# Moving the placement of dtu by one decay, loading all expert rows at once, and 32 matmuls ahead of the last stage of a Mamba and mixture-of-experts kernel

## The chip, the cores and the metric

The kernel runs on one core of a Trainium2 chip (trn2). The metric is the device time of one execution in microseconds. Three executions of the kernel before took 2603.61, 2604.18 and 2603.98 us, so the median is 2603.98. All data are float32.

## What is computed

Input `x` has 32 sequences of 128 tokens with 128 features. Four things follow one another; cut to what matters:

```python
# 1. adapter per sequence (its language picks the weights), then layer norm
x1 = norm(x + relu(x @ W1[id] + b1[id]) @ W2[id] + b2[id]) * gamma[id] + beta[id]
# 2. four Mamba layers, d_inner 256, state 16
for i in range(4):
    xs, z = split(layer_norm(x1) @ Wi.T)
    u = silu(causal_conv4(xs) + cb)
    dt, B, C = split(u @ Wx.T);  dt = softplus(dt @ Wdt.T + bdt)
    h[t] = exp(dt[t] * A) * h[t-1] + dt[t] * u[t] * B[t];  y[t] = h[t] . C[t]
    x1 = ((y + u * Dp) * silu(z)) @ Wo.T + x1
x = x + x1
# 3. dense experts: 8 gated by fside, one shared, each (silu(x Wg) * (x Wu)) Wd
y = (1 - sg) * sum_e p[e] * expert_e(x) + sg * shared(x)
# 4. sparse experts, top 2 of 8 by y @ wg, capacity 1024 rows each
out = x + g1 * ffn_e1(y) + g2 * ffn_e2(y)      # ffn: gelu(row @ w_gate) @ w_down
```

## The kernel before

`mega` calls three phases: `wave_phase` (1 and 2, and the dense experts of half of the tokens woven in), `dense_phase` (the dense experts of the other half, and the routing), and `sparse_phase` (4). Each is one block of code with a program for each of the engines PE, ACT, DVE, POOL and SP (SP only issues DMAs). Engines run their own program in the order in which it is written, and meet through counting semaphores. At the end of a block there is a drain of each engine and a semaphore round of all.

**The wave.** Tokens are in 8 groups of four sequences (512 columns). An iteration `i` (0 to 31) is one layer of one group, and has 16 steps `k`, each for two of the 16 states of one half of the channels. In a step ACT makes the decays (`decay`, L715: two exponentials, at most four steps ahead of the scans), DVE multiplies `dtu` in PSUM by B (`input_term`, L882) and scans (`scan_step`, L893), POOL multiplies by C (`weigh_states`, L1030), and PE adds the states up in PSUM (`sum_states`, L452). In between, by the tables `PE_AT`, `ACT_AT` and `POOL_AT`, which name a piece of work for a step `k`, the next iteration is prepared. On ACT the pieces of a step stand ahead of its decay. `dtu` (dt times u) of the next iteration is made by POOL at step 11 (`time_input`, L1012), and in the first half (iterations below `RING0` = 13) ACT copies its two channel halves into the banks `psT[0]` and `psT[1]` (`place_dtu`, L683): half 0 as `dtu0` at step 15 of the iteration before, half 1 as `dtu1` at step 1 of its own. Half 0's bank has been free since the middle of the iteration before, half 1's only after its last scan. The copy of half 0 waits for POOL's `dtu`. DVE's input term of step 0 waits for the copy.

**The end of the dense phase.** After the last group's experts come its routing on PE and DVE (`post`, `ranks`, `slots`), a small matmul into `psN` (L1324), and on POOL eight indirect DMAs (`scatter`, L1217) that write the last group's rows into `disp` in DRAM. `disp` has two arrays (first and second choice) of 8 experts by 1024 rows of 132 numbers: the token, its index and its weights.

**The sparse phase.** SP loads both arrays' rows of an expert into `dx[0]` and `dx[1]` (`load_rows`, L1518 and L1520; 528 KB each, expert 0's in halves), in a ring of three experts (`NDX`), so expert `e` from 3 on waits until expert `e-3` has been weighed (`evac`). Experts 0 and 1 have their weights loaded in the dense phase; the others' stand in the ring of two (`load_weights`, L1525 and L1526). An expert is two halves of 512 rows. For each half DVE picks rows from the two arrays (`pick`, L1621), PE transposes (`turn`, L1560), DVE copies (`turned`, L1633), PE multiplies by `w_gate` (`up`, L1570), ACT takes the gelu (L1607), PE multiplies by `w_down` (`down`, L1578), and DVE scales by the routing weight into `eos` (`weigh`, L1644). POOL then adds the rows to `out` in DRAM by eight indirect DMAs an expert (L1546), 128 rows each, and waits at the start of an expert until all DMAs of the expert before have landed (`added`), as two experts can add to the same token.

## Time and profile before

| | us |
|---|---|
| median of three runs | 2603.98 |
| the profiled execution | 2603.44 |
| its span, first to last instruction | 2601.7 |
| PE busy (matmuls) | 2318.5 (89%) |
| DVE busy | 2055.6 (79%) |
| POOL busy | 2045.6 (79%) |
| ACT busy | 1555.7 (60%) |
| DVE scans, 512 of 2.283 us | 1165.7 |
| POOL products by C, 512 of 2.36 us | 1205.4 |
| ACT decays, 1024 of 0.708 us | 667.4 |
| POOL scatters into `out`, 64 of 1.555 us | 99.5 |

Busy shares are means over stages with different limits: the wave lasts to 2047 us, the dense phase to about 2437, the sparse phase to the end. PE's busy time counts matmuls that are pipelined, with modelled ends. In rows of a timeline the numbers are the start, the duration of the merged instructions, the engine, the line, the operation with its output and inputs, how many instructions are merged (x), and in brackets the idle time of the engine before them and what ended it.

### The profile page before, as it was taken

To read this page: it belongs to the slowest core of one execution; us is meant where nothing else is said; L and a number is where in the kernel's file an instruction comes from. 1 tells how busy PE (TensorE), PEld (TensorE's weight loads), DVE (VectorE), ACT (ScalarE), POOL (GpSimd) and SP (SyncE) were. 2 spreads that over 40 slices of the span, in tenths; PEclk is the share of its full clock that TensorE was granted. 3 is DMA by queue.
4 is the path that set the end of the run, shared out by engine and by line. 5 is a ranking of instruction groups with operands and counts; after the bars stand their busy time and mean duration, and the time that the engine had idled before them with its cause. 6 is when DMAs were issued, how large, how long until landed. Compare 5 with 4: busy or idle time off the path is not lost. (4 is left out here: it accounts for less than half of the span.)

```text
span 2601.7 us, 22564 instructions
## 1 busy us (share of the span) xinstructions
PE 2318.5 (89%) x6064; PEld 1023.4 (39%) x6064; DVE 2055.6 (79%) x2028; ACT 1555.7 (60%) x2432; POOL 2045.6 (79%) x1269
## 2 busy tenths in 40 slices
PE   6588888888888999999999999999998899999594
PEld 4233333333333333343443333333333344444373
DVE  4799999999999999999999999999999343333221
ACT  3576777776777677777766767777765223222221
POOL 4599999999998899999999999999999332321366
PEclk9799999999999999999999999999999999999797
DMA  7466545654445766776667676766676400100353
GB/s 222 186 217 209 182 161 184 215 206 160 144 163 186 256 243 233 238 244 228 230 231 240 220 238 234 244 231 227 234 245 220 144 21 10 36 9 9 89 123 36
DMA packets 216929, 464.96 MB, mean 179 GB/s; under 512 B 29468, under 2 KB 109154, under 8 KB 216802
## 3 DMA queue, kind: packets, MB, share of 16 engines
q1 hardware_dynamic: 204818, 455.30, 51.3%
q0 software_dynamic: 11264, 7.98, 2.0%
q8 instruction: 49, 0.80, 0.1%
q14 instruction: 78, 0.64, 0.1%
q10 hardware_dynamic: 720, 0.23, 0.1%
HBM read 440.00 MB, written 23.99 MB: 178 GB/s over the span
## 5 line engine op out<-in xcount | busy, mean ns | idle before, releaser
L893 DVE TENSOR_TENSOR_SCAN hh<-decays,psdB 128x1024 f32<-128x1024 f32 x512 | 1165.7, 2283 | 58.9 <-ACT decays L715 18.6
L1030 POOL TENSOR_TENSOR products<-hh,Clo 128x1024 f32<-128x1024 f32 x408 | 961.4, 2360 | 112.1 <-DVE hh L893 111.1
L452 PE MATMUL psY<-products,ident 128*128 128x512 f32 x1708 | 831.9, 607 | 120.4 <-POOL products L1030 73.1
L715 ACT ACTIVATE decays<-dt,Acur 128x508 f32<-128x508 f32 x1024 | 667.4, 708 | 6.0 <-DVE hh L893 5.6
L452 PEld LDWEIGHTS psY<-products,ident 128*128 128x128 f32 x1708 | 311.5, 191 | 567.8 <-issue 350.4
L882 DVE TENSOR_TENSOR psdB<-psT,Blo 128x1024 f32<-128x1024 f32 x395 | 484.2, 1226 | 29.7 <-DMA Blo<-rows 1.8
L1458 DVE TENSOR_TENSOR ac<-sg,d_bank 128x512 f32<-128x512 f32 x135 | 92.8, 688 | 225.1 <-PE d_bank L1308 207.1
L432 PE MATMUL psW<-xnT,wcur 128*128 128x512 f32 x496 | 229.1, 604 | 41.8 <-DMA diag<-diags_l 22.9
L1030 POOL TENSOR_TENSOR products<-hh,late 128x1024 f32<-128x1024 f32 x104 | 244.0, 2366 | 18.3 <-PE psY L452 18.3
L1356 ACT ACTIVATE sg<-d_bank 128x512 f32<-128x512 f32 x135 | 80.6, 597 | 244.7 <-PE d_bank L1304 244.6
L1034 POOL TENSOR_TENSOR products<-products 128x512 f32<-128x512 f32 x170 | 215.7, 1269 | 13.3
L1208 POOL TENSOR_TENSOR xw<-x1T,wbc 128x512 f32<-128x512 f32 x27 | 28.1, 1045 | 181.2 <-PE d_bank L1308 181.1
L493 PE MATMUL psdB<-late,fw 128*128 128x512 f32 x306 | 161.7, 610 | 7.3 <-DVE late L915 6.9
L432 PEld LDWEIGHTS psW<-xnT,wcur 128*128 128x128 f32 x496 | 94.5, 193 | 171.9 <-issue 109.2
L485 PE MATMUL psdB<-h_res,fw 128*128 128x512 f32 x306 | 160.0, 605 | 0.1
L500 PE MATMUL psT<-late,fw 128*128 128x512 f32 x306 | 159.7, 604 | 0.0
L1546 POOL DMA_INDIRECT out<-eos,home x64 | 99.5, 1555 | 65.7 <-issue 34.9
L689 ACT ACTIVATE yg<-psY 128x512 f32<-128x512 f32 x64 | 38.2, 597 | 181.7 <-PE psY L452 181.7
L915 DVE TENSOR_TENSOR late<-late,psdB 128x512 f32<-128x512 f32 x153 | 103.8, 679 | 36.1 <-PE psdB L493 36.1
L1217 POOL DMA_INDIRECT disp<-tok,idx x64 | 62.7, 979 | 88.0 <-DVE idx L1436 70.2
L1308 PE MATMUL d_bank<-xw,wgu 128*128 128x512 f32 x256 | 130.7, 592 | 0.0
L1271 PE MATMUL d_bank<-ac,wdn 128*128 128x512 f32 x256 | 129.4, 592 | 0.0
(215 smaller groups left out, 2975.0 us busy)
## 6 DMA issues: line engine op xcount, KB each, us to landing
Blo<-rows SPq DMA_DIRECT2D x280, 512.0 KB, 5.7
Clo<-rows SPq DMA_DIRECT2D x280, 512.0 KB, 4.9
late<-rows SPq DMA_DIRECT2D x104, 512.0 KB, 6.1
wcur<-taps_l SPq DMA_DIRECT2D x31, 512.0 KB
fw<-in_Wg SPq DMA_DIRECT2D x36, 256.0 KB, 5.2
fw<-in_Wu SPq DMA_DIRECT2D x36, 256.0 KB, 4.5
fw<-in_Wd SPq DMA_DIRECT2D x36, 256.0 KB, 5.2
disp<-fw SPq DMA_DIRECT2D x16, 528.0 KB, 7.1
```

The costliest lines, as they stand in the source:

```text
L432: ins = pe.matmul(at[:, :], lhsT=wcur[:, k, c * 128:(c + 1) * 128], rhs=xnT[:, :, k:k + T], start=(k == 0), stop=(k == NTAP - 1))
L452: ins = pe.matmul(psY[:, :], lhsT=ident[:, :], rhs=gg[k % NGB][:, j, :], start=False, stop=(k % NK == NK - 1 and j == last - 1))
L485: pe.matmul(psG, lhsT=fwg[:, e % NXW, f * 128:(f + 1) * 128], rhs=flat(n // NST), start=True, stop=True).then_inc(gated, 1)
L493: pe.matmul(psU, lhsT=fwu[:, e % NXW, f * 128:(f + 1) * 128], rhs=xw[:, e % NXW, :], start=True, stop=True).then_inc(upped, 1)
L500: pe.matmul(psD[:, :], lhsT=fwd[:, e % NXW, f, :], rhs=sg[:, n % NSLG, :], start=(n % NST == 0), stop=(n % NST == NST - 1 or n == NSTR - 1 ...
L715: ins = act.activation(dA[k % NDA][:, j, :, 1:T], dt[i % 2][:, c, :, 1:T], ACT.Exp, scale=Acur[i % 2][:, s:s + 1])
L882: dve.tensor_tensor(dB[b][:, :, :], (psT[c] if i < RING0 else psT[0])[:, :].unsqueeze(1).broadcast_to([128, 2, TOK]), tile(Blo, Bhi, slot( ...
L893: dve.tensor_tensor_scan(out=hh[k % NHB][:, :, :].rearrange("p c t -> p (c t)"), data0=dA[k % NDA][:, :, :, :].rearrange("p c q t -> p (c ...
L1030: ins = pool.tensor_tensor(gg[k % NGB][:, :, :], hh[k % NHB][:, :, :], tile(Clo, Chi, slot(i, s)), ALU.mult)
L1034: ins = pool.tensor_tensor(gg[k % NGB][:, 0, :], gg[k % NGB][:, 0, :], gg[k % NGB][:, 1, :], ALU.add)
L1271: ins = pe.matmul(psD[:, :], lhsT=down_w(h, r // NF, r % NF), rhs=ac[r % NAC][:, :], start=(r == 0), stop=(r == NST - 1))
L1308: pe.matmul(psU[r % 2][:, :], lhsT=up_w(h, e, f), rhs=xw[(NE1 * h + e) % NXW][:, :, :], start=True, stop=True).then_inc(upped, 1)
```

## The change

There are three parts. In the first half of the wave the copy of `dtu`'s half 0 moves on ACT from step 15 of the iteration before to step 1 of its own, ahead of the other pieces of that step, that is, behind the decays of steps 15 and 0. At the end of PE's program in the dense phase 32 matmuls are added, with the identity as weights and 512 columns of `wgu`, alternately into two banks of which nothing is read after; they wait until ACT's last silu has read these. In the sparse phase `dx` has room for all eight experts, SP issues all loads of rows without a wait and the weights of experts 2 to 7 behind them, and rows are counted by four semaphores: expert 0, expert 1, experts 2 and 3, experts 4 to 7 (`BATCH`), each complete only with its last load. Five semaphores are merged or dropped on the way: the two of the softplus, the two of the deviation, and `weighted`, in whose place `homed` is waited for.

```diff
@@ -41,8 +41,8 @@
 AHEAD = {"x0": 2, "x1": 1, "z0": 1, "z1": 1, "bcdt": 1, "dt0": 1, "dt1": 1, "outT": -1, "out": -1, "T": 2}
 PE_AT = {0: ["x1"], 1: ["z0"], 2: ["z1"], 4: ["bcdt"], 6: ["dt0"], 7: ["dt1"], 8: ["outT"], 9: ["out"], 12: ["T"], 14: ["x0"]}
 SUM_FIRST = (15,)
-ACT_AT = {1: ["params", "dtu1", "norm"], 2: ["turn0"], 4: ["sums1", "x0"], 5: ["x1"], 6: ["z0"], 7: ["z1", "silu"], 8: ["bcdt"], 10: ["turn1"], 11: ["dt0"],
-          12: ["dt1", "sums0", "softplus"], 13: ["outT"], 14: ["added"], 15: ["centre", "dtu0"]}
+ACT_AT = {1: ["dtu0", "params", "dtu1", "norm"], 2: ["turn0"], 4: ["sums1", "x0"], 5: ["x1"], 6: ["z0"], 7: ["z1", "silu"], 8: ["bcdt"], 10: ["turn1"], 11: ["dt0"],
+          12: ["dt1", "sums0", "softplus"], 13: ["outT"], 14: ["added"], 15: ["centre"]}
 GIVEN = {4: 0, 9: 5, 13: 8}
 POOL_AT = {1: ["gate1"], 6: ["rstd"], 10: ["dt"], 11: ["dtu"], 12: ["gate0"]}
 G_AT = [-11, -9, -7, -6, -5, -4, -2, 0, 1]
...
@@ -667,9 +667,9 @@
                     if what == "softplus":
                         whole = soft[:, :, :].rearrange("p c t -> p (c t)")
                         act.wait_ge(wfree, W["dt1", t] + 1)
-                        act.activation(whole, whole, ACT.Exp, scale=-1.0).then_inc(exp_ok, 1)
-                        act.wait_ge(exp_ok, t)
-                        act.activation(whole, whole, ACT.Ln, bias=1.0).then_inc(ln_ok, 1)
+                        act.activation(whole, whole, ACT.Exp, scale=-1.0).then_inc(soft_ok, 1)
+                        act.wait_ge(soft_ok, 2 * t - 1)
+                        act.activation(whole, whole, ACT.Ln, bias=1.0).then_inc(soft_ok, 1)
 
                 def place_dtu(t, c):
                     if t == 0 and c == 0:
@@ -808,8 +808,8 @@
                                 copy_sums(i, 0)
                             if what == "dtu1" and i < RING0:
                                 place_dtu(i, 1)
-                            if what == "dtu0" and i + 1 < RING0:
-                                place_dtu(i + 1, 0)
+                            if what == "dtu0" and 0 < i < RING0:
+                                place_dtu(i, 0)
                             if what == "turn0" and i >= RING0:
                                 place_dtu(i, 0)
                             if what == "turn1" and i >= RING0:
@@ -995,14 +995,14 @@
-                    pool.tensor_scalar(negm[:, :], mv[:, :, 0], -1.0, None, ALU.mult).then_inc(rs1, 1)
-                    pool.wait_ge(rs1, t + 1)
-                    pool.tensor_tensor(rstd[:, :], vare[:, :], K["nhalf"][:, :], ALU.pow).then_inc(rs2, 1)
-                    pool.wait_ge(rs2, t + 1)
+                    pool.tensor_scalar(negm[:, :], mv[:, :, 0], -1.0, None, ALU.mult).then_inc(rs, 1)
+                    pool.wait_ge(rs, 2 * t + 1)
+                    pool.tensor_tensor(rstd[:, :], vare[:, :], K["nhalf"][:, :], ALU.pow).then_inc(rs, 1)
+                    pool.wait_ge(rs, 2 * t + 2)
...
-                    pool.wait_ge(ln_ok, t)
+                    pool.wait_ge(soft_ok, 2 * t)
@@ -1322,6 +1322,9 @@
                 post(NG - 1)
                 ranks(NG - 1)
                 pe.matmul(psN, lhsT=ones[:, :], rhs=cnt[:, G, 0, :], start=True, stop=True).then_inc(counted, 1)
+                pe.wait_ge(silued, CR + NST * NDT)
+                for r in range(32):
+                    pe.matmul(psG[r % 2][:, :], lhsT=ident[:, :], rhs=wgu[:, 0, 0, :], start=True, stop=True)
 
             @block.scalar
             def _(act):
@@ -1480,17 +1483,18 @@
         NHT = CAP // 512
         HC = NCH // NHT
         wg, wd, w_ld = K["ewg"], K["ewd"], K["ew_ld"]
-        NDX, NEO = 3, 3
-        dx = [[sb(f"dx{c}_{p}", [128, NCH, RW]) for p in range(NDX)] for c in range(2)]
+        NEO = 3
+        BATCH = [0, 1, 2, 2, 3, 3, 3, 3]
+        dx = [[sb(f"dx{c}_{p}", [128, NCH, RW]) for p in range(NE)] for c in range(2)]
         dT = [sb(f"dT{b}", [128, 512]) for b in range(2)]
         ht = [sb(f"ht{b}", [128, NF, 512]) for b in range(2)]
         eos = [sb(f"eos{p}", [128, NCH, D]) for p in range(NEO)]
         home = [sb(f"home{e}", [128, NCH], u32) for e in range(NE)]
         bank = [ctx.enter_context(nc.psum_tensor(f"e_bank{b}", [128, 512], f32)) for b in range(8)]
         psT, psH, psE = bank[0:2], bank[2:6], bank[6:8]
-        x_ld, x_first = [sem(f"x_ld{p}") for p in range(NDX)], sem("x_first")
-        picked, homed, weighted, trans, copied, upped, gelud, downed, evac, added = (
-            sem(n) for n in "picked homed weighted trans copied upped gelud downed evac added".split())
+        x_ld, x_first = [sem(f"x_ld{b}") for b in range(4)], sem("x_first")
+        picked, homed, trans, copied, upped, gelud, downed, evac, added = (
+            sem(n) for n in "picked homed trans copied upped gelud downed evac added".split())
         tokens = out.rearrange("b t d -> (b t) d")
 
         def at_least(eng, sm, v):
@@ -1510,14 +1514,12 @@
                 for p in range(2):
                     sp.wait_ge(K["scat"][p], 16 * 2 * NSEQ // 2)
                 def load_rows(e):
-                    p = e % NDX
-                    at_least(sp, evac, CR + NHT * (e - 2))
                     lo = HC if e == 0 else 0
                     if e == 0:
                         for c in range(2):
-                            sp.dma_start(dx[c][p][:, 0:HC, :], A["disp"][c, e, 0:CAP // NHT].rearrange("(n p) d -> p n d", p=128)).then_inc(x_first, 16)
+                            sp.dma_start(dx[c][e][:, 0:HC, :], A["disp"][c, e, 0:CAP // NHT].rearrange("(n p) d -> p n d", p=128)).then_inc(x_first, 16)
                     for c in range(2):
-                        sp.dma_start(dx[c][p][:, lo:NCH, :], A["disp"][c, e, 128 * lo:CAP].rearrange("(n p) d -> p n d", p=128)).then_inc(x_ld[p], 16)
+                        sp.dma_start(dx[c][e][:, lo:NCH, :], A["disp"][c, e, 128 * lo:CAP].rearrange("(n p) d -> p n d", p=128)).then_inc(x_ld[BATCH[e]], 16)
 
                 def load_weights(e):
                     p = e % 2
@@ -1525,11 +1527,10 @@
                     sp.dma_start(wg[p][:, :], A["w_gate"][e]).then_inc(w_ld[p], 16)
                     sp.dma_start(wd[p][:, :, :], A["w_down"][e].rearrange("(t p) d -> p t d", p=128)).then_inc(w_ld[p], 16)
 
-                for e in range(NE + 1):
-                    if e < NE:
-                        load_rows(e)
-                    if e > 2:
-                        load_weights(e - 1)
+                for e in range(NE):
+                    load_rows(e)
+                for e in range(2, NE):
+                    load_weights(e)
 
             @block.gpsimd
             def _(pool):
@@ -1553,7 +1554,7 @@
                     pe.sem_inc(sm, CR)
 
                 def turn(e, c):
-                    h, p = NHT * e + c, e % NDX
+                    h, p = NHT * e + c, e
                     pe.wait_ge(picked, CR + h + 1)
                     at_least(pe, copied, CR + h - 1)
                     for q in range(HC):
@@ -1613,16 +1614,16 @@
                 dve.sem_inc(picked, CR)
 
                 def pick(e, c):
-                    p, at = e % NDX, slice(HC * c, HC * (c + 1))
+                    p, at = e, slice(HC * c, HC * (c + 1))
                     if e == 0 and c == 0:
                         dve.wait_ge(x_first, 32)
                     elif c == (1 if e == 0 else 0):
-                        dve.wait_ge(x_ld[p], 32 * (e // NDX + 1))
+                        dve.wait_ge(x_ld[BATCH[e]], 32 * BATCH.count(BATCH[e]))
                     dve.copy_predicated(dx[1][p][:, at, 0:D + 1], K["first"][:, e, at].unsqueeze(2).broadcast_to([128, HC, D + 1]), dx[0][p][:, at, 0:D + 1]).then_inc(picked, 1)
 
                 def address(e):
-                    x = e % NDX
-                    dve.copy_predicated(dx[1][x][:, :, D + 2], K["first"][:, e, :], dx[0][x][:, :, D + 1]).then_inc(weighted, 1)
+                    x = e
+                    dve.copy_predicated(dx[1][x][:, :, D + 2], K["first"][:, e, :], dx[0][x][:, :, D + 1])
                     dve.wait_ge(picked, CR + NHT * (e + 1))
                     dve.tensor_copy(home[e][:, :], dx[1][x][:, :, D]).then_inc(homed, 1)
 
@@ -1635,14 +1636,14 @@
                 def weigh(e, c):
                     h, p = NHT * e + c, e % NEO
                     if c == 0:
-                        dve.wait_ge(weighted, e + 1)
+                        dve.wait_ge(homed, e + 1)
                         if e >= NEO:
                             dve.wait_ge(added, 16 * NCH * (e - NEO + 1))
                     for lo, n in ((q, 1) for q in range(HC)) if last(h) else ((0, HC),):
                         at = slice(HC * c + lo, HC * c + lo + n)
                         dve.wait_ge(downed, CR + h + 1 + lo)
                         dve.tensor_tensor(eos[p][:, at, :], sums(h, lo, n).rearrange("p (q d) -> p q d", q=n),
-                                          dx[1][e % NDX][:, at, D + 2].unsqueeze(2).broadcast_to([128, n, D]), ALU.mult).then_inc(evac, 1)
+                                          dx[1][e][:, at, D + 2].unsqueeze(2).broadcast_to([128, n, D]), ALU.mult).then_inc(evac, 1)
 
                 pick(0, 0)
                 turned(0, 0)
```

## Rows read from the trace of the kernel before

**Rows 1.** The chain of work that ended last, its shares by line.

```profile
by line: POOL out L1546 0.7%; issue 0.4%; POOLq L1546 0.0%
```

**Rows 2.** Timeline of POOL in the sparse phase: first or last scatters of experts.

```profile
2455.82 1.60 POOL L1546 DMA_INDIRECT out<-eos,home  x1 [24.36 <-DVE eos L1644]
...
2469.55 1.54 POOL L1546 DMA_INDIRECT out<-eos,home  x1 [0.30 <-issue]
2475.02 1.54 POOL L1546 DMA_INDIRECT out<-eos,home  x1 [3.92 <-DVE eos L1644]
...
2492.16 1.54 POOL L1546 DMA_INDIRECT out<-eos,home  x1 [2.48 <-DMA out<-eos,home]
...
2522.18 1.54 POOL L1546 DMA_INDIRECT out<-eos,home  x1 [0.30 <-issue]
2529.36 1.54 POOL L1546 DMA_INDIRECT out<-eos,home  x1 [5.64 <-issue]
```

**Rows 3.** Instructions of the dense block's line: op, count, ns min/median/max, start us.

```profile
L1169 PEldq DRAIN  x1: 1450/1450/1450, 2417.9 to 2417.9; - x1
...
L1169 POOLq DRAIN  x1: 11830/11830/11830, 2424.9 to 2424.9; - x1
```

**Rows 4.** Timeline of SP (issues of DMAs) in the sparse phase.

```profile
2437.06 0.92 SPq L1518 DMA_DIRECT2D dx<-disp  x2
...
2522.35 0.99 SPq L1520 DMA_DIRECT2D dx<-disp  x2
```

**Rows 5.** Timeline of PE, end of the dense phase to the end.

```profile
2413.74 0.63 PE L1285 MATMUL d_bank<-ident,h_res 128*128 128x128 f32 x4
...
2441.69 1.12 PE L1560 MATMUL e_bank<-ident,dx 128*128 128x128 f32 x4 [22.38 <-DVE dx L1621]
2443.68 5.87 PE L1570 MATMUL e_bank<-dT,ewg 128*128 128x512 f32 x8 [0.88 <-DVE dT L1633]
...
2453.91 3.60 PE L1570 MATMUL e_bank<-dT,ewg 128*128 128x512 f32 x8
...
2477.20 7.03 PE L1570 MATMUL e_bank<-dT,ewg 128*128 128x512 f32 x16
...
2564.76 1.06 PE L1578 MATMUL e_bank<-ewd,ht 128*128 128x128 f32 x8
```

**Rows 6.** Timeline of PE's weight loads, one of either phase.

```profile
2401.68 0.19 PEld L1271 LDWEIGHTS d_bank<-ac,wdn 128*128 128x128 f32 x1 [0.24 <-issue]
...
2446.37 0.34 PEld L1570 LDWEIGHTS e_bank<-dT,ewg 128*128 128x128 f32 x1 [0.52 <-issue]
```

**Rows 7.** Stretches: length, busy us (x) of PE, PEld, DVE, ACT, POOL; clock, DMA share, GB/s.

```profile
2417.00:2418.00 1.00, 0.11 (x1) 0.14 (x1) 0.86 (x6) 0.06 (x1) 0.00 (x0) 0.69 0.00 0
...
2438.00:2449.00 11.00, 6.44 (x12) 3.01 (x13) 2.19 (x3) 1.82 (x4) 0.00 (x0) 0.54 1.12 291
...
2448.00:2449.00 1.00, 1.00 (x4) 0.44 (x3) 0.00 (x0) 0.34 (x2) 0.00 (x0) 0.95 1.12 272
...
2570.00:2572.00 2.00, 0.00 (x0) 0.00 (x0) 0.00 (x0) 0.00 (x0) 1.70 (x2) 0.75 0.35 33
```

**Rows 8.** Wave: DVE's waits to 794 us; timelines of ACT and DVE at a boundary.

```profile
DVE hh L893 <- ACT decays L715: 18.6, 13, 2.5
...
627.31 0.60 ACT L683 ACTIVATE psT<-dtu 128x512 f32<-128x512 f32 x1 [2.84 <-POOL dtu L1012]
...
632.87 0.60 ACT L683 ACTIVATE psT<-dtu 128x512 f32<-128x512 f32 x1 [2.28 <-DVE hh L893]
...
642.06 0.60 ACT L689 ACTIVATE yg<-psY 128x512 f32<-128x512 f32 x1 [4.24 <-PE psY L452]
...
681.82 0.60 ACT L683 ACTIVATE psT<-dtu 128x512 f32<-128x512 f32 x1 [2.86 <-POOL dtu L1012]
...
632.67 1.21 DVE L882 TENSOR_TENSOR psdB<-psT,Blo 128x1024 f32<-128x1024 f32 x1
```

**Rows 9.** Timeline of DVE in the sparse phase: expert 2's first pick.

```profile
2463.43 0.75 DVE L1621 COPY_PREDICATED dx<-first,dx 128x516 f32<-128x516 int32 x1
```

More of the change, by code:

```diff
@@ L188, in wave_phase @@
         first_use = {"x0": dB[0][:, 0, :], "x1": dB[0][:, 1, :], "bcdt": dB[0][:, 0, :], "dt0": dB[0][:, 1, :]}
-        names = ("wcur_ld wready wfree dbu da scan prod half red stat moments rs1 rs2 rstd_ok centred skipped par_ok kept_ok exp_ok ln_ok dt_ok dtu_ok placed silu_ok "
+        names = ("wcur_ld wready wfree dbu da scan prod half red stat moments rs rstd_ok centred skipped par_ok kept_ok soft_ok dt_ok dtu_ok placed silu_ok "
                  "ycopied ygated gave moved cleared zero zeroed x_ld x1_ok x_st gated gfree sg_ok scaled upped acted downed sum_ok").split()
-        (wcur_ld, wready, wfree, dbu, da, scan, prod, half, red, stat, moments, rs1, rs2, rstd_ok, centred, skipped, par_ok, kept_ok, exp_ok, ln_ok, dt_ok, dtu_ok, placed, silu_ok,
+        (wcur_ld, wready, wfree, dbu, da, scan, prod, half, red, stat, moments, rs, rstd_ok, centred, skipped, par_ok, kept_ok, soft_ok, dt_ok, dtu_ok, placed, silu_ok,
          ycopied, ygated, gave, moved, cleared, zero, zeroed, x_ld, x1_ok, x_st, gated, gfree, sg_ok, scaled, upped, acted, downed, sum_ok) = (sem(n) for n in names)
```

## The prediction

> **What bounds the kernel now.** Three stages follow one another in the trace of one core: the wave (0 to 2047 us, four state-space layers with half of the dense experts woven in), the dense stage (to 2420.8 us) and the sparse stage (to the end). I first read the chain of work that ended last. It only reaches back over the last 33 us and holds nothing but POOL's scatters into `out` [rows 1]. So I went on by stage, asking which engine has no slack.
>
> In the sparse stage the timeline of POOL decides. Each expert takes eight indirect DMAs, one every 1.85 us, then a wait of about 2.5 us for the last of them to land, before the next expert may begin. Experts 1 and 2 start 17.14 us apart, and from expert 2 on no start waits for PE or DVE. Two starts are out of this step. Expert 1's waited 3.92 us for DVE's `eos`: expert 0's last scatter began at 2469.55, so with 1.54 us of its own and 2.5 of landing POOL would have been ready at 2473.6, and it started at 2475.02, 1.4 us later. Expert 4's came after 5.64 us idle, where expert 2's had 2.48 [rows 2].
>
> Between dense and sparse lies a gap. The rows of the dense block's line are the engines' drains and semaphores at its end: all engines wait there for one another. PE's drain ended at 2419.3, POOL's lasted 11.83 us, to 2436.75, and ended last [rows 3]. SP's first load of rows was issued at 2437.06, 0.31 us behind it [rows 4], and the first transposes ran at 2441.69, after 22.38 us without work on PE [rows 5].
>
> In the first half of the wave DVE is the bound. One iteration is 54.5 us (ACT's copy of `dtu` at 627.31 has its like at 681.82), and over 13 iterations DVE lost 18.6 us to decays, about 1.37 us an iteration, apart from one wait of 11.9 us in the first iteration [rows 8].
>
> **Part 1: `dtu0` behind the first decay.** Nothing is added: twelve copies of 0.60 us change place. Before, ACT stood 2.84 us at step 15 until POOL had made `dtu`, placed it at 627.31, and only then made decay 15 and the next iteration's decay 0, four activations of 0.7 us. Now these can run first, from 624.5 to about 627.1 (their buffers are free, since ACT may be four steps ahead of the scans), and the copy lands at 627.3 to 627.9 as before, since POOL's product ends at the same time. DVE's first input term that reads it started at 632.67, so 4.8 us of cover are left. The wait that is gone returns at once: behind it ACT copies `dtu1`, which has to wait for the last scan of the iteration (it stood 2.3 us for it, to 632.87), and then at 642.06 it stands 4.24 us for PE's sums [rows 8]. The decay that DVE does wait for (1.37 us, step 7) comes behind both. So the part is worth **0**, with -0.5 to +0.5 us as bounds: the two copies shown waited 2.84 and 2.86 us for POOL, 12 times that difference is 0.24, and I double it. The merged semaphores (one for the two steps of softplus, one for the deviation) keep each wait, and cost nothing.
>
> **Part 2: 32 matmuls ahead of the block's end.** They stand in PE's queue behind the last dense matmul. Their only wait, for the last silu, is long satisfied, so they start at 2419.3. PE's drain is behind them, and so is the barrier, and behind that SP's first load, DVE's pick and PE's own first transposes. A float32 matmul of 512 columns is two instructions in this trace; they follow one another by 0.43 us in the dense stage (a weight load of 0.19 and 0.24 to the next), 0.86 us a matmul, and at half clock by 0.34 + 0.52 = 0.86 us, 1.72 us a matmul [rows 6]. At 2419.3 the clock is low: it fell between 2417 and 2418, three us after the last long burst (to 2414.4), and after the gap it came back at 2448.1, that is 6.4 us after the first transposes and 4.4 us after the first dense matmuls [rows 5, 7]. I take 5.4 us low: 3.1 matmuls in it, then 28.9 by 0.86 = 24.8 us, 30.2 us in all. They end at 2449.5, the barrier opens with them and no longer with POOL, and SP loads at 2449.8 in place of 2437.06: **+12.7 us**. Bounds: with the full clock from the first on 32 by 0.86 = 27.5 us, +10.0; with 6.4 us low 30.7 us, +13.2. The cover that I looked for is POOL's scatter and drain, which hide the matmuls only to 2436.75, that is 17.4 us of the 30.2.
>
> What the matmuls can give back is clock. The first burst of expert 0 ran low: four transposes in 1.12 us, of which full clock saves about half, and the eight instructions of the first `up` in 5.87 against 3.60 [rows 5], 2.8 us with both. But the barrier, the load and the pick still lie between: 2441.69 less 2436.75 is 4.9 us without work on PE [rows 3, 5]. At the very end of the kernel the clock fell about 5 us after PE's last matmul (2565.8) [rows 5], at the block's end three us after the burst [rows 5, 7], so here it falls before or during the first work, and has to be earned again. I take **-0.3 us**, with -2.8 (held throughout) and +0.5 (falls a little later than now and so lasts longer) as ends.
>
> The Trainium skill (TensorE: Matmul & The Clock Gate, Why this matters for your kernels) advises matmuls ahead of the work that counts to bring the engine to full rate. By that rule alone the sum would have -2.8 us here in place of -0.3; the rows on the fall speak against it, and it stays as rival (a).
>
> **Part 3: all rows at once.** The 14 loads of 528 KB and the four halves are issued without a wait, about 0.5 us each, 8.65 MB. They move at 291 GB/s [rows 7], so they take 30 us with a latency of 1, and POOL's first scatters, 18.8 us after SP's first load [rows 2, 4], now run beside the second half of them. The first rows are still first in the queue and cost the same. Experts 2 and 3 share one count and are complete after 4.2 MB, 15 us behind the first load; their first pick came 26 us behind it [rows 9]. Experts 4 to 7 are complete at 31 us, and needed only two experts later than these. Expert 2's weights now stand behind all rows, and land at about 33 us; its first `up` ran at 2477.20, 40 us behind [rows 5]. None of that is late. What it removes is the collision at 2522: SP issued expert 7's rows at 2522.35, with expert 6's weights behind them, 0.17 us after POOL began expert 3's last scatter, and that landed 3.1 us later than the others [rows 2, 4]. The weights (512 KB of the 1.57 MB) stay at this place, so I take three quarters of it, **-2.4 us**, with -3.1 and 0 as ends. In the other direction the row loads may now hold back expert 0's last scatter by the same 3.1 us, of which 1.4 are covered by the wait for `eos`: 0 to +1.7, and I take 0, as it comes 33 us after the first load and the rows need 30. The dropped semaphore on the weights' copy adds a wait for an address that DVE has made itself earlier: nothing.
>
> The Trainium skill (DMA: Bandwidth & Descriptors, Queues, rings and completion order) says that each DMA engine serves its queues in turn, packet by packet. By it a scatter would be slowed beside a load but never stand behind all of it, and the term for expert 4 would be nearer to 0, for a sum 2.4 us higher; the row of 5.64 us shows at least that the last landing does get later.
>
> **Sum.** 0 + 12.7 - 0.3 - 2.4 = +10.0 us on the profiled execution's 2603.44 us (its span of 2601.70 and 1.74 around it) is 2613.4. The median of the runs is 0.54 us above the profiled one, so 2614.0 us.
>
> **Rivals.**
> (a) The clock is held over the gap: 2614.0 - 2.5 = 2611.5. For it: a gap of 4.9 us is a little shorter than the 5 us at the end of the kernel. Against: the 3 us at the block's end. 13%.
> (b) The row loads disturb the scatters of expert 0 and the weights still collide at 2522: + 2.4 + 1.7, 2618.1. 14%.
> (c) The matmuls do not hold the barrier (say, the drain doesn't wait for them). PE would still be busy to 2449.5 while its transposes could start at 2441.7: +7.8, with the clock held -2.8, with part 3 -2.4: 2606.6, no change that can be measured. PE's drain of 1.45 us, which lasted until its last matmul had ended, speaks against it. 5%; together with smaller gains of part 3 that I don't see, 8%.
> (d) The other side: **faster through the wave.** ACT has 2.84 us more at each of twelve boundaries. If they reached step 7, DVE's wait of 1.37 us would go: -16.4, 2597.6. It decides where ACT's queue no longer meets a wait for others between steps 15 and 7; it meets two (2.3 and 4.24 us), which is why I give it 5%, and 1% for other ways to be faster.
> (e) The clock stays low through all 32 matmuls: 32 by 1.72 = 55.0 us, 24.8 more than summed, 2638.8. Dense matmuls have brought it back within 4.4 us [rows 5, 7]. 2%.
>
> **How the numbers follow.** The forecast itself holds the other 57%. It and (a) and (b) lie between 2609 and 2619. The ends of all terms at once would be +4.1 and +15.4; all at one end is unlikely, and the range of 2608.5 to 2619 leaves out (c), (d), (e) and little more. About 0.2% (5.2 us) can be told from no change in a measurement of this kernel: slower by more than that holds for the forecast, (a), (b) and (e), 86%; within it (c), 8%; faster (d), 6%.
>
> **What would show it.** In the profile after: the drain of PE at the dense block's end is the last and ends near 2449, and POOL's ended 12 us earlier; SP's first load stands 0.3 us behind it. The 64 new instructions fill PE from 2419 on, spaced 0.85 us for the first five, then 0.43. The transposes of expert 0 start 5 us after they end, and the granted clock shows a second fall near them. POOL's idle time before expert 4 shrinks from 5.6 to about 3.2 us. In the wave DVE's period stays at 54.50 us, with the same 1.37 us at step 7, and the wait for POOL's `dtu` on ACT is shorter by the two decays. I am wrong if the dense block ends at 2437 as before, if the period of the wave moves by 0.1 us or more, or if POOL's scatters of expert 0 are spread out by the row loads.

## The result, and the profile after

The changed kernel takes 2615.57 us (median of six runs, 2613.69 to 2617.10), the kernel before 2603.80 beside it (2602.64 to 2604.47). The ratio is 1.0043, interval 1.0033 to 1.0054: 11.8 us slower. The forecast was 2614.0, in a range of 2608.5 to 2619.0. The medians and ratios below leave out one execution, of the kernel called `n17_gap4`, which took 6637.39 us; nothing here explains it.

The profiled execution took 2616.36 us. The head of its page (busy us, share of the span, instructions) shows the same busy times as the table of before, but on PE, with 38.9 us more:

```profile
span 2614.6 us, 22692 instructions
PE 2357.4 (90%) x6128; PEld 1040.8 (40%) x6128; DVE 2055.2 (79%) x2028; ACT 1555.3 (59%) x2432; POOL 2045.8 (78%) x1269
```

Of these 38.9 us the new matmuls are 30.3. Another 6.6 lie in the first 500 us, where PE was busy for 411.04 us against 404.40 before at a granted clock of 0.95 against 0.97, with the same work. The window of after (stretch, length, busy us of PE, PEld, DVE, ACT, POOL; clock, DMA share, GB/s):

```profile
0.00:500.00 500.00, 411.04 (x1031) 178.05 (x1032) 432.39 (x465) 332.89 (x542) 425.75 (x264) 0.95 0.56 195
```

The timeline of PE in the profile after answers to [rows 5]:

```profile
2420.62 0.54 PE L1324 MATMUL d_bank<-r_cnt,ones 128*128 128x8 f32 x2
2421.02 30.29 PE L1327 MATMUL d_bank<-wgu,ident 128*128 128x512 f32 x64
2456.17 1.12 PE L1561 MATMUL e_bank<-ident,dx 128*128 128x128 f32 x4 [4.86 <-DVE dx L1622]
2458.16 6.45 PE L1571 MATMUL e_bank<-dT,ewg 128*128 128x512 f32 x8 [0.87 <-DVE dT L1634]
...
2468.98 3.60 PE L1571 MATMUL e_bank<-dT,ewg 128*128 128x512 f32 x8
```

The 32 matmuls (64 instructions) take 30.29 us, and the first transposes of the sparse stage wait until they are through. Why they wait stands in the instructions of the block's line (op, count, ns min/median/max, start us), the answer to [rows 3], and in SP's timeline, the answer to [rows 4]:

```profile
L1169 POOLq DRAIN  x1: 11823/11823/11823, 2426.8 to 2426.8; - x1
L1169 PEldq DRAIN  x1: 7888/7888/7888, 2443.4 to 2443.4; - x1
L1169 SPq EVENT_SEMAPHORE  x1: 17/17/17, 2451.5 to 2451.5; - x1
```

SP:

```profile
2451.63 0.92 SPq L1520 DMA_DIRECT2D dx<-disp  x2
...
2537.41 0.34 SPq L1527 DMA_DIRECT2D ewg<-in_w_gate  x1
```

POOL's drain ends at 2438.6 and now PE's is the last: 2443.4 + 7.89 = 2451.3. SP's release follows at 2451.5 and its first load at 2451.63. Before, POOL's drain was last.

The timeline of POOL in the profile after, first scatters of experts 0, 1, 2, 4 and 5 and (fourth row) the last of expert 3, answers to [rows 2]:

```profile
2470.89 1.60 POOL L1547 DMA_INDIRECT out<-eos,home  x1 [37.58 <-DVE eos L1645]
...
2490.08 1.54 POOL L1547 DMA_INDIRECT out<-eos,home  x1 [3.90 <-DVE eos L1645]
...
2507.33 1.54 POOL L1547 DMA_INDIRECT out<-eos,home  x1 [2.57 <-DMA out<-eos,home]
...
2537.33 1.54 POOL L1547 DMA_INDIRECT out<-eos,home  x1 [0.30 <-issue]
2542.26 1.54 POOL L1547 DMA_INDIRECT out<-eos,home  x1 [3.39 <-issue]
...
2559.41 1.54 POOL L1547 DMA_INDIRECT out<-eos,home  x1 [2.48 <-issue]
```

Experts 0 and 1 keep their distance (19.19 us), and expert 4's idle time fell from 5.64 to 3.39 us.

Cut at four instants, the difference of the two spans is accounted for. "Counted" is the matmul at L1324, "load" SP's first load, "e0" and "e7" the first scatters of these experts. Rows of [rows 2, 4] and this one of PE's timeline give the first columns of before; the others are from the same timelines.

```profile
2418.77 0.54 PE L1324 MATMUL d_bank<-r_cnt,ones 128*128 128x8 f32 x2
```

| us | counted at | counted to load | load to e0 | e0 to e7 | e7 to the end |
|---|---|---|---|---|---|
| before | 2418.77 | 18.29 | 18.76 | 124.53 | 21.35 |
| after | 2420.62 | 31.01 | 19.26 | 122.50 | 21.21 |
| difference | +1.85 | +12.72 | +0.50 | -2.03 | -0.14 |

The sum is 12.9 us, the difference of the spans. The first 1.85 us can't be ascribed to the change for sure: in the twelve profiles of the kernels below the same instant lies between 2418.8 and 2421.6, 2419.55 and 2420.25 in the two whose wave is as before. In after's profile they arise for the most part in one place: the scan that began at 153.96 us before begins at 153.28, and the one at 172.58 at 173.96, 2.05 us lost between. There the clock was low in part, and PE took 3.01 us in place of 1.98 for sums at 138 us. Such a step (2.05 to 2.3 us) stands in 8 of the 11 profiles with part 1 and in none of the three without. So a small cost of part 1 at this place isn't excluded by the profiles; the medians of `p1_dtu` below limit it. From "counted" to the end the change costs 31.01 + 19.26 + 122.50 + 21.21 less the same of before, 11.05 us. I use the difference of this stretch below for every kernel, and call it **the difference behind the dense stage**.

### The profile page after: what moved, and what is told of

It is laid out like the page before. It is cut to its first block and busy times, and to the rows that moved or that the text cites. A ratio compares the mean times of both kernels' runs of the same rounds, so it can differ in the third digit from the quotient of the medians.

```text
span 2614.6 us, 22692 instructions
## 1 busy us (share of the span) xinstructions
PE 2357.4 (90%) x6128; PEld 1040.8 (40%) x6128; DVE 2055.2 (79%) x2028; ACT 1555.3 (59%) x2432; POOL 2045.8 (78%) x1269
## 5 line engine op out<-in xcount | busy, mean ns | idle before, releaser
L893 DVE TENSOR_TENSOR_SCAN hh<-decays,psdB 128x1024 f32<-128x1024 f32 x512 | 1165.8, 2283 | 55.9 <-ACT decays L715 19.8
L1034 POOL TENSOR_TENSOR products<-products 128x512 f32<-128x512 f32 x170 | 215.7, 1269 | 13.3
```

Of the source, the lines that this page charges most:

```text
L893: dve.tensor_tensor_scan(out=hh[k % NHB][:, :, :].rearrange("p c t -> p (c t)"), data0=dA[k % NDA][:, :, :, :].rearrange("p c q t -> p (c ...
L1034: ins = pool.tensor_tensor(gg[k % NGB][:, 0, :], gg[k % NGB][:, 0, :], gg[k % NGB][:, 1, :], ALU.add)
```

## The experiments

My theory before the first four: only the matmuls cost time, they hold the barrier, and each beyond POOL's cover costs 0.86 us; the rows give back a little; the wave is untouched. The rivals were a gain or loss in the wave hidden in the total, and a loss by the rows.

**One part at a time.** `p1_dtu` has part 1 alone (the new `ACT_AT` and the merged semaphores), `p2_matmuls` the 32 matmuls alone, `p3_rows` part 3 alone, and `p13_no_matmuls` is the changed kernel with this edit:

```diff
-                pe.wait_ge(silued, CR + NST * NDT)
-                for r in range(32):
-                    pe.matmul(psG[r % 2][:, :], lhsT=ident[:, :], rhs=wgu[:, 0, 0, :], start=True, stop=True)
```

> Part 1 alone on the kernel before: dtu0 behind the first decay, with the merged semaphores. Theory: worth nothing, 0 within 0.5 us of the kernel before; DVE's period in the wave stays 54.50 us and ACT's wait for POOL's dtu shrinks from 2.85 to about 0.4 us, coming back in its wait for the scan. Rival: the dense stage of the changed kernel ended 1.85 us later in its profile than before, and if part 1 causes that, this kernel is 1.5 to 2 us slower in the median. Rival on the other side: 16 us faster, if ACT's 2.8 us at each boundary reached the decay of step 7.

> Part 2 alone: the 32 matmuls. Theory: PE's drain, not POOL's, ends the dense block, and SP's first load stands 31.0 us behind the last small matmul in place of 18.3: +12.7 us, and the clock gives back between 0 and 0.5 us or takes as much: +12.2 to +13.3 us on the median. Rival: if the clock were held over the gap of 4.9 us, +10 us. Rival: if the matmuls only cost together with the loads of part 3, under +5 us.

> Part 3 alone: all rows at once. Theory: POOL's idle time before expert 4 shrinks from 5.6 to 3.4 us, as in the changed kernel, all else as before: -2.2 us. Rival: the row loads beside expert 0's scatters take it back: 0. Rival: the collision moves to another expert: 0.

> The changed kernel without the 32 matmuls (parts 1 and 3). Theory: -2.2 us against the kernel before, the same as part 3 alone, so that the matmuls alone make the changed kernel the slower one. Rival: if part 1 costs 1.5 to 2 us in the wave, the sum is 0 to -0.7 us.

Measured, each against the same 2605.43 us of the kernel before on their chip:

| | median | difference | ratio | behind the dense stage |
|---|---|---|---|---|
| `p1_dtu` | 2605.72 | +0.3 | 0.9998 [0.9989, 1.0007] | +0.2 |
| `p2_matmuls` | 2618.75 | +13.3 | 1.0050 [1.0036, 1.0064] | +13.2 |
| `p3_rows` | 2603.86 | -1.6 | 0.9993 [0.9984, 1.0002] | -0.8 |
| `p13_no_matmuls` | 2604.29 | -1.1 | 0.9995 [0.9986, 1.0004] | -0.7 |

(A ratio here is fitted over all runs, so it can differ from that of the medians by some hundredths of a per cent.) The whole loss is the matmuls', and the parts add up: 0.3 + 13.3 - 1.6 = 12.0 against 11.8. The three other intervals all hold 1, so of parts 1 and 3 the medians alone show no effect. In `p2_matmuls` SP's first load stands 30.84 us behind "counted", as in after.

Part 3 was worth less alone than its step for expert 4 says. The timeline of POOL in `p3_rows`, first scatters of experts 4 and 5:

```profile
2528.74 1.54 POOL L1544 DMA_INDIRECT out<-eos,home  x1 [3.43 <-issue]
...
2546.91 1.59 POOL L1544 DMA_INDIRECT out<-eos,home  x1 [3.55 <-issue]
```

SP's weights for experts 6 and 7:

```profile
2523.86 0.34 SPq L1524 DMA_DIRECT2D ewg<-in_w_gate  x1
...
2538.75 0.34 SPq L1524 DMA_DIRECT2D ewg<-in_w_gate  x1
```

Expert 4's idle time falls as forecast, but expert 5's rises from 2.50 to 3.55 us: the weights issued at 2538.75 came 3.07 us ahead of expert 4's last scatter at 2541.82. `p13_no_matmuls` (3.15) and `n64` (3.79) lose there too. But in after, `n16`, `n16_gap5` and `gap5_alone` the same load stands 3.07 to 3.08 us ahead of the same scatter, and POOL stood idle for 2.48 to 2.59 us alone. So the same edit gives 2 us or under 1 between the first scatters of experts 0 and 7 (2.0 in these four, 0.8 in `p3_rows`, `p13_no_matmuls` and `n64`), and the offset between load and scatter, which is the same, doesn't say which. What does is open.

**How many matmuls are free.** `n16` and `n64` are the changed kernel with another count. They test the price of 0.86 us a matmul and the cover of about 17 us.

```diff
-                for r in range(32):
+                for r in range(16):        # n64: range(64)
```

> The changed kernel with 16 matmuls in place of 32. Theory: the cover ahead of the barrier is POOL's drain, which ends 17.4 us after PE's last small matmul; 16 matmuls take 5.4 us low for 3.1 and 12.9 by 0.86 = 11.1 us, 16.5 us in all, so they fit under it. SP's first load is back at 18.3 us behind the last small matmul, the clock falls again in the gap, and the time is that of the kernel without them: about 2 us below the kernel before. Rival: any matmul there costs (the clock, the drain, the power), and the time is in the middle between the kernel without them and the one with 32, +5 us.

> The changed kernel with 64 matmuls. Theory: the 32 more stand wholly in front of the barrier and at full clock, 32 by 0.86 = 27.5 us more than the changed kernel: 2643 us. SP's first load stands 58.5 us behind the last small matmul. Rival: if something beside their own duration holds the barrier (the clock, the loads), the step is not 0.86 us a matmul.

`n16` took 2603.30 against 2604.51 us (0.9992 [0.9983, 1.0001]). Timeline of PE and the drains in `n16`:

```profile
2421.58 16.46 PE L1327 MATMUL d_bank<-wgu,ident 128*128 128x512 f32 x32
2444.57 1.12 PE L1561 MATMUL e_bank<-ident,dx 128*128 128x128 f32 x4 [6.53 <-DVE dx L1622]
```

The drains:

```profile
L1169 POOLq DRAIN  x1: 11805/11805/11805, 2427.3 to 2427.3; - x1
L1169 PEldq DRAIN  x1: 7890/7890/7890, 2430.2 to 2430.2; - x1
```

Sixteen end at 2438.0, one us ahead of POOL's drain, and "counted to load" is 18.26 us: the barrier doesn't move. They are free, and worth nothing either: the transposes again take 1.12 us, at low clock, since 6.5 us without a matmul lie between. `n64` gave 2644.82 us in a single run. "Counted" in PE's timeline and the first load in SP's:

```profile
2420.68 0.54 PE L1324 MATMUL d_bank<-r_cnt,ones 128*128 128x8 f32 x2
...
2478.98 0.92 SPq L1520 DMA_DIRECT2D dx<-disp  x2
```

Its "counted to load" is 58.30 us, 27.3 more than with 32: 0.853 us each, with none of it hidden. Its difference behind the dense stage is +39.5 us; the single run is 40.3 above the median of before. That the matmuls hold the barrier once they outlast POOL's drain is shown by 16 and 17 (18.26 and 18.28, as before) against 32 (31.01); what one more costs, by 32 against 64.

**Matmuls on either side of the barrier.** The clock falls within the barrier, so I put some behind it, in the 5 us in which PE waits for the first rows. `n16_gap5` has 16 ahead and five behind, `n17_gap4` 17 and 4, `gap5_alone` none ahead and five behind.

```diff
-                for r in range(32):
+                for r in range(16):        # n17_gap4: 17; gap5_alone: the loop is left out
...
+                for r in range(5):         # n17_gap4: 4
+                    pe.matmul(psE[r % 2][:, :], lhsT=K["ident"][:, :], rhs=K["fw"][:, 0, :], start=True, stop=True)
                 turn(0, 0)
```

> As with 16 matmuls, and five more at the head of PE's program in the sparse stage, behind the barrier, on 512 columns of a buffer of the dense stage, into the banks of the down products. At full clock they take 4.3 us of the gap of 4.6 us. Theory: the clock falls in the gap because PE idles in it, so now it is held: the first transposes take 0.60 and the first up 3.60 us, 2.8 us less, on top of part 3: -4.5 to -5 us against the kernel before. Rival: the clock is low when they start, then they take 8.6 us and the first transposes come 4 us late: 0 to +2 us against the kernel before.

> 17 matmuls ahead of the barrier and four behind it, with parts 1 and 3. With 16 and five the clock fell at 2440.5, after 1.95 us without work on PE round the barrier, and the five took 6.2 us. 17 end about 0.3 us before POOL's drain, and PE idles 1.1 us. Theory: that is short enough for the clock to hold; four take 3.6 us, the transposes and the first up run at full clock and do not wait for the matmuls, and POOL's first scatter comes 16.2 us after SP's semaphore at the barrier (18.9 before, 18.1 with 16 and five): -4 to -5 us against the kernel before. Rival: the clock falls with 1.1 us idle too, and the time is that of 16 and five, -2.4 us.

> Parts 1 and 3 without matmuls ahead of the barrier, and five behind it, in the gap itself. Theory: the clock is low there, so the five take 8.6 us from about 2437.6 us on, or a little less if it comes back before their end, and the first transposes start 3 to 4 us later than without them; the first up is then at full clock (3.6 us, 2.3 less, with the transposes 2.8): 0 to +1.5 us against parts 1 and 3 alone. Rival: the earlier start of work brings the clock back soon enough to pay for them: -1 us against parts 1 and 3 alone.

| | median | before | ratio | load to e0 | e0 to e7 | behind the dense stage |
|---|---|---|---|---|---|---|
| `n16_gap5` | 2602.06 | 2604.51 | 0.9988 [0.9979, 0.9997] | 17.94 | 122.54 | -2.8 |
| `n17_gap4` | 2602.67 | 2604.95 | 0.9992 [0.9983, 1.0001] | 16.01 | 124.77 | -2.5 |
| `gap5_alone` | 2601.16 | 2604.95 | 0.9989 [0.9980, 0.9998] | 18.02 | 122.52 | -2.7 |

"Load to e0" (before 18.76) holds the arrival of the first rows, the transposes and the first `up`; the clock decides how long these two take. Timelines of PE in `n16_gap5`, then in `n17_gap4`:

```profile
2440.33 6.23 PE L1584 MATMUL e_bank<-fw,ident 128*128 128x512 f32 x10 [1.94 <-PEq L1169]
2446.39 0.60 PE L1561 MATMUL e_bank<-ident,dx 128*128 128x128 f32 x4
2447.87 3.67 PE L1571 MATMUL e_bank<-dT,ewg 128*128 128x512 f32 x8 [0.87 <-DVE dT L1636]
```

`n17_gap4`:

```profile
2438.99 3.67 PE L1584 MATMUL e_bank<-fw,ident 128*128 128x512 f32 x8 [0.98 <-PEq L1169]
2443.07 0.66 PE L1561 MATMUL e_bank<-ident,dx 128*128 128x128 f32 x4 [0.40 <-DVE dx L1624]
2444.60 3.67 PE L1571 MATMUL e_bank<-dT,ewg 128*128 128x512 f32 x8 [0.88 <-DVE dT L1636]
```

With 1.94 us idle between the two groups the clock fell at about 2440.5, 0.2 us behind the start of the second (0.53 in the window from 2440.5 to 2441). The five matmuls brought it back, but took 6.23 us, so that the first transposes ran 2.0 us behind DVE's pick, where before they ran at once. The first `up` began 1.4 us later than before and was 2.2 us shorter. With 0.98 us idle it was held, as the windows of `n17_gap4` show (stretch, length, busy us of PE, PEld, DVE, ACT, POOL; granted clock, DMA share, GB/s), and the full 2.75 us came:

```profile
2438.00:2440.00 2.00, 1.02 (x4) 0.56 (x4) 0.00 (x0) 1.28 (x1) 0.00 (x0) 1.00 0.13 19
2440.00:2446.00 6.00, 4.72 (x15) 2.01 (x14) 2.20 (x3) 0.27 (x1) 0.00 (x0) 1.00 1.11 303
```

And yet it is no faster than the others. What it won it lost on POOL. First scatters of experts 1, 3 and 4 in `n17_gap4`, and SP's weights:

```profile
2475.19 1.54 POOL L1547 DMA_INDIRECT out<-eos,home  x1 [5.35 <-DMA out<-eos,home]
...
2510.92 1.54 POOL L1547 DMA_INDIRECT out<-eos,home  x1 [3.91 <-issue]
...
2528.25 1.54 POOL L1547 DMA_INDIRECT out<-eos,home  x1 [2.56 <-issue]
```

SP's loads of weights in `n17_gap4`, the first and the fourth:

```profile
2466.21 1.65 SPq L1527 DMA_DIRECT2D ewg<-in_w_gate  x1
...
2506.18 0.34 SPq L1527 DMA_DIRECT2D ewg<-in_w_gate  x1
```

Expert 0's scatters now come sooner behind the first load, so that the last rows and expert 2's weights are still moving when its last one is to land. Expert 1 waits 5.35 us, for the landing and no longer for `eos`. The collision of expert 4 is gone, and expert 3 has it instead. `gap5_alone` shows that the matmuls ahead of the barrier aren't needed for what five behind it bring: "load to e0" is 18.02 against 17.94. Its -3.8 us in the medians is more than its trace explains (-2.7), but its ratio is -2.9 us, with an interval of -5.2 to -0.5; that its lead over `n16_gap5` is real isn't shown.

**The weights.** Two kernels, both without matmuls, try to move the weights out of the way: `weights_at_once` gives experts 2 to 7 buffers of their own and loads all weights behind the rows, `ring4` has a ring of four. `ring4_n17_gap4` adds the 17 and 4.

```diff
                 def load_weights(e):
-                    p = e % 2
-                    at_least(sp, evac, CR + NHT * (e - 1))
+                    p = e                                      # weights_at_once
...
+                    p = e % 4                                  # ring4
+                    sp.wait_ge(evac, CR + NHT * max(e - 3, 1))
```

> Parts 1 and 3 without matmuls, and the weights of experts 2 to 7 loaded at once behind the rows as well, into buffers of their own, so that SP issues nothing while POOL scatters, from about 2465 us on. Theory: what is left of the late landing ahead of expert 4 (3.4 us idle against 2.5) is the weights of one expert, 512 KB, so it goes and all starts from expert 2 on are 2.5 us idle apart: 0.9 us less than without it, -3 us against the kernel before. Rival: the 11.8 MB last 40 us, 7 us beyond expert 0's last scatter, which then lands late by up to 3.1 us, of which 1.4 are covered: 0 to -1.3 us against the kernel before, and expert 2's weights keep PE waiting.

> Parts 1 and 3 without matmuls, and the experts' weights in a ring of four: those of 2, 3 and 4 are loaded once expert 0 is weighed, 5, 6 and 7 one expert after the other behind it, three experts ahead. Nothing is loaded any more while expert 3's last scatter lands (at 2537 us in the changed kernel), nor while expert 0's does. Theory: the idle time ahead of expert 4 falls from 3.4 to 2.5 us, the one ahead of expert 1 stays 3.9 with DVE's eos as its end: -0.9 us against parts 1 and 3 alone. Rival: the 1.5 MB behind expert 0 bring its landing late as with all weights at once (5.5 us idle ahead of expert 1), +0.7 us.

> Everything together: parts 1 and 3, 17 matmuls ahead of the barrier and four behind, the ring of four for the weights. Theory: the sum of the single steps, -2.2 (part 3), -2.8 (clock held), -0.9 (no weights at expert 3's landing): -5 to -6 us against the kernel before, the fastest of all. Rival: the clock falls with 1.1 us idle, then -3 us.

| | median | before | ratio | idle before experts 1, 3, 4 | behind the dense stage |
|---|---|---|---|---|---|
| `weights_at_once` | 2603.62 | 2604.51 | 0.9999 [0.9990, 1.0008] | 5.50, 2.58, 2.62 | +0.2 |
| `ring4` | 2605.22 | 2604.95 | 1.0000 [0.9992, 1.0009] | 5.06, 3.82, 2.57 | +0.5 |
| `ring4_n17_gap4` | 2602.43 | 2604.95 | 0.9991 [0.9982, 1.0000] | 5.58, 3.59, 2.65 | +0.1 |

The expectations for these failed at one point in all three: the loads that no longer meet a late expert meet expert 0. In `ring4` I had reckoned that the wait for `evac` would keep the loads away from these scatters. It couldn't: it ends when DVE has weighed expert 0, and that is well ahead of POOL's last scatter of it (2472.10). The 18 issues of rows took 27 us, not 9, but that only put the loads off from 2465.3 to 2466.64. Timelines of SP, then of DVE in `ring4`, the weighing of expert 0's second half:

```profile
2440.42 26.11 SPq L1522 DMA_DIRECT2D dx<-disp  x16
2466.64 1.92 SPq L1532 DMA_DIRECT2D wg<-in_w_gate  x1
...
2470.54 0.70 SPq L1532 DMA_DIRECT2D ewg<-in_w_gate  x1
```

DVE:

```profile
2464.61 0.69 DVE L1650 TENSOR_TENSOR eos<-e_bank,dx 128x512 f32<-128x512 f32 x1 [2.73 <-PE e_bank L1584]
```

POOL in `ring4`, first scatters of experts 1 and 3:

```profile
2478.71 1.54 POOL L1552 DMA_INDIRECT out<-eos,home  x1 [5.06 <-DMA out<-eos,home]
...
2514.63 1.54 POOL L1552 DMA_INDIRECT out<-eos,home  x1 [3.82 <-issue]
```

Three experts' weights, 1.5 MB, were issued within 5 us beside expert 0's scatters, and what is won at expert 4 is lost at experts 1 and 3. `weights_at_once` has lost less idle time (1.6 us at expert 1 against 3.0 won at expert 4), but single scatters took up to 2.05 us in place of 1.54, 1.2 us more in all and 0.9 of it in expert 4's, while nothing was loaded; why is open. In the profile of `ring4_n17_gap4` the clock, held in `n17_gap4`, fell during the first `up`, which took 5.37 us: PE had stood still for 1.06, 1.12 and 0.88 us between the end of the 17 and this `up`, and in `n17_gap4` for 0.98, 0.40 and 0.88. Its rows also came 0.7 us later, so of the 2.4 us by which its "load to e0" is longer 1.7 are the clock's. This profiled execution, at 2605.85 us, is the second slowest of its eleven, so its +0.1 and the medians' -2.5 don't speak of the same thing. How often the clock is held with 17 and 4 stays open.

## Why the prediction was right

**Part 2, the barrier: +12.7, measured 12.72.** Every link held. The matmuls started with the clock low; it rose at 2426.2, 5.2 us behind their start (5.4 in the forecast), and they took 30.29 us (30.2). PE's drain was the last and POOL's ended 12.7 us earlier. SP's load stands 0.3 us behind that drain (0.31 before). The starting point in the sum, 2419.3, was that of the profile of before; in after's profile it is 1.85 us later, which moves both ends and not their difference. The cover of 17.4 us held for 17 matmuls (17.38 us in `n17_gap4`), and `n64` shows the price of one by itself. This term carries the forecast.

**Part 2, the clock: -0.3, measured +0.50.** The sign was wrong, and it came out at the upper bound (-2.8 to +0.5). The -0.3 itself was no reading of a row, only a choice between "falls before or during the first work" and the clock held. What came is what the prediction gave for its upper end: it fell later than before and so lasted longer. The windows of after:

```profile
2452.00:2453.00 1.00, 0.00 (x0) 0.00 (x0) 0.00 (x0) 0.92 (x1) 0.00 (x0) 1.00 0.30 35
2453.00:2454.00 1.00, 0.00 (x0) 0.00 (x0) 0.00 (x0) 0.00 (x0) 0.00 (x0) 0.76 1.03 299
2454.00:2456.00 2.00, 0.00 (x0) 0.00 (x0) 0.63 (x1) 0.00 (x0) 0.00 (x0) 0.50 1.06 295
...
2463.00:2464.00 1.00, 1.00 (x2) 0.34 (x1) 0.00 (x0) 0.34 (x1) 0.00 (x0) 0.62 1.21 298
```

It fell at about 2453.5, 2.2 us behind PE's last matmul and 2.7 us ahead of the first transposes, so these and most of the first `up` ran at 1.2 GHz (1.12 and 6.45 us; 1.12 and 5.87 in [rows 5]). Then it rose 7.6 us behind the first transposes, where [rows 5, 7] had 6.4. So the 32 matmuls bought nothing, and rival (a), the clock held over the gap, is out: not even in `n16_gap5` did it last much over 1.94 us of idle time at this place. The Trainium skill (TensorE: Matmul & The Clock Gate, Why this matters for your kernels) advises matmuls as a warm-up, there ahead of a benchmark. The traces agree where such matmuls stand behind the barrier: with the 17 ahead of it and four behind, `n17_gap4` shows 2.75 us, and with five behind alone `gap5_alone` shows 0.74. For those ahead of it alone "load to e0" rose by 0.50 us in after, 0.48 in `p2_matmuls`, 0.23 in `n16` and 0.22 in `n64`. In `n16` that isn't the clock's: its first `up` was 0.26 us shorter than before (5.61) and its rows came 0.49 later. By the lengths of transposes and first `up` the term lay between -0.3 and +0.6 us in the four, so -0.3 was within what can come and +0.5 is no fixed cost.

**Part 3: -2.4, measured -2.25 at expert 4.** The size is about right in this profile, but -2.25 isn't what the part is worth by itself. In `p3_rows`, `p13_no_matmuls` and `n64` 0.65 to 1.3 us are lost again at expert 5, which the forecast hadn't looked for; after was spared, in this profile at least. A step that failed without cost: the issues of the rows were put at 0.5 us each, 9 us, and took 26 us from the first load to expert 2's weights (2477.86 in after); its first `up` was still on time. That expert 0's landing would not be late held too: expert 1 waited 3.90 us, for `eos`. But its slack of 1.4 us is thin: 2.7 us less in "load to e0" used it up in `n17_gap4`. By the Trainium skill (DMA: Bandwidth & Descriptors, Queues, rings and completion order) each DMA engine serves its queues in turn, packet by packet, by which a scatter would be slowed and not blocked. The runs agree in so far as landings beside 0.5 MB of weights came at most 1.4 us later, less than the 1.8 us that this load needs at the 291 GB/s of [rows 7] (an estimate); the 3.1 us of before stood beside three times as many bytes. The prediction's reading of it, a term for expert 4 nearer to 0, did not come true.

**Part 1: 0, measured +0.3 with 0 well inside the interval (-2.9 to +1.8).** The wait moved as told. Timeline of ACT at a boundary in the profile after, and its waits to 794 us (us in total, times, longest), answering to [rows 8]:

```profile
625.83 2.53 ACT L715 ACTIVATE decays<-dt,Acur 128x508 f32<-128x508 f32 x4
628.78 0.60 ACT L683 ACTIVATE psT<-dtu 128x512 f32<-128x512 f32 x1 [0.42 <-POOL dtu L1012]
...
634.33 0.60 ACT L683 ACTIVATE psT<-dtu 128x512 f32<-128x512 f32 x1 [4.70 <-DVE hh L893]
...
643.52 0.60 ACT L689 ACTIVATE yg<-psY 128x512 f32<-128x512 f32 x1 [4.24 <-PE psY L452]
```

The waits:

```profile
ACT psT L683 <- DVE hh L893: 55.7, 12, 5.0
...
DVE hh L893 <- ACT decays L715: 19.8, 13, 2.5
```

The four decays are made before the copy, which waits 0.42 us in place of 2.84; the next copy waits 4.70 in place of 2.28, 2.42 more, and the wait for PE's sums behind it is still 4.24. DVE's own wait for decays, the one that would make the wave shorter, is 19.8 us against 18.6, and its period stays at 54.50 (its waits for the decays at step 7 end at 606.57 and 661.07). A cost of up to 1.8 us lies within the interval, so the step between 154 and 173 us isn't ruled out as this part's. Rival (d) needed that wait to go. (c) is out by PE's drain, (e) by the 30.29 us, and of (b) its first half, expert 0's landing late, came true in `n17_gap4` and `weights_at_once`, not here.

**The size.** +11.8 in the medians against +10.0: 11.05 is in the trace behind the dense stage, so 1.05 us are the two small terms (0.8 clock, 0.2 rows), and the other 0.7 is inside the interval of the ratio (8.6 to 14.1 us); no run says what it is. The hit is owed to the barrier's term. That the small ones came out only 1.05 us off together is in part luck: the clock's term varied by 0.9 us between four profiles, and part 3 gave 0.8 or 2.0 us. Two figures of the prediction were summed wrongly, to no effect: with part 1's own bounds the ends of all terms are +3.6 and +15.9, and 18.6 us over 13 iterations are 1.43 us each.

## What to carry to other kernels

Matmuls that are to keep the clock up count against whatever the next barrier waits for: find which engine's drain ends last, and put in no more than it covers (here 17.4 us, 0.86 us each), or put them behind the barrier, where the engine waits for data anyway (here the first scatter came 0.7 to 2.75 us sooner; with part 3 these kernels gained about 3 us of 2605 at most). When a landing is on the path, list what else is in flight at each landing before moving loads: here `p3_rows`, `n17_gap4` and both kernels with more buffers for weights freed one expert's landing and had another late. PE's period of 14.89 us (which times the weights) and POOL's of 17.05 drift against one another, so every shift changes which landing meets a load. A wait for what an engine has computed is not a wait for the scatter behind it: in `ring4` they lay 6.8 us apart. Before a few us in one profile are explained, cut the span at an instant ahead of the edit: 1.85 of the 12.9 us here lie ahead of the first new matmul.

## What the runs showed of the hardware

- POOL's drain at the block's end is what the matmuls hide behind. Its record is 11.8 us long in every profile, but begins while the eight scatters into `disp` still run (2426.8 in after, where they last from 2423.37 to 2433.30) and ends 5.25 to 5.35 us behind the last of them. PE's drain doesn't end before its queued matmuls do, and with them queued its own record is 7.9 us long.
- Issuing isn't free when much is in flight: 16 row loads of 528 KB or less took SP 25 to 27 us to issue, and the first weights behind them 1.65 to 2.33 us in place of 0.34.
- POOL's idle time while an expert's last scatter lands depends on when a load is issued beside it, taking the weights' issue against the last scatter's start over all profiles: 2.3 us behind it or more, 2.5 to 2.6 us; 0.7 behind, 3.8 to 3.9; 0.4 behind, 3.6; 0.1 to 0.2 behind, 3.3 to 3.5; 3.07 ahead, 2.5 to 2.6 in five cases and 3.15 to 3.8 in three; with rows or more weights at once, 5.1 to 5.6. A load of 0.5 MB issued by SP costs such a landing up to 1.4 us, and in five of the cases nothing.
- TensorE's clock fell from 2.4 to 1.2 GHz 0.2 us behind a stretch of 1.94 us without a matmul (`n16_gap5`), and stayed at 2.4 over stretches of 0.98, 0.40 and 0.88 us with short work between (`n17_gap4`); behind 1.06, 1.12 and 0.88 us it fell (`ring4_n17_gap4`). One execution each.
